# Delta rule: decay differences of four items by one bf16 product of three-part splits

## The reference, cut to what matters

```python
g = -jnp.exp(A_log) * jax.nn.softplus(a + dt_bias)
gc = jnp.cumsum(gT.reshape(Bs, NV, N, CHUNK), axis=-1)
diff = gc[..., :, None] - gc[..., None, :]
decay = jnp.exp(jnp.where(tril, diff, 0.0)) * tril
A = -(jnp.einsum('bhnid,bhnjd->bhnij', k_beta, kc) * decay) * strict
attn = jnp.einsum('bhid,bhjd->bhij', q_i, k_i) * dec_i
```

## Time and profile before

| | |
|---|---|
| median of three executions | 2367.83 us (2364.08 to 2368.61) |
| the profiled execution, its own time | 2367.39 us |
| its span | 2365.6 us |
| phase c in it | about 717 to 1967 us |
| DMA, mean over the span | 30 GB/s |

### The profile page before, as it was taken

How to read it: one execution, slowest core, us unless ns; L and a number is a source line. 1 busy time by engine, 2 the same in 40 slices (tenths; PEclk the granted TensorE clock), 3 DMA queues, 4 the chain that set the end, 5 groups by cost and what they waited for, 6 DMA issues and landing times. The chain is left out here.

```text
span 2365.6 us, 27433 instructions
## 1 busy us (share of the span) xinstructions
PE 2013.7 (85%) x10306; PEld 1495.7 (63%) x10306; DVE 1455.8 (62%) x3243; ACT 879.5 (37%) x1540; POOL 154.4 (7%) x143
## 2 busy tenths in 40 slices
PE   6988987998994978899988999889998893787786
PEld 5867866554553667576675766757667582465464
DVE  3667665323222566867668666786666854767666
ACT  2433433111113444353544535535354431333242
POOL 2011011000001000000000000000000002011110
PEclk8989898999996889999999999999999996787787
DMA  3000000400001110201102011020110202000000
GB/s 131 6 14 10 6 5 30 163 1 9 0 1 67 36 36 14 61 16 36 37 14 57 20 37 36 15 60 17 36 36 14 49 1 72 7 12 15 7 5 5
DMA packets 129108, 70.62 MB, mean 30 GB/s; under 512 B 107152, under 2 KB 119504, under 8 KB 127984
## 3 DMA queue, kind: packets, MB, share of 16 engines
q1 hardware_dynamic: 128976, 68.86, 10.2%
HBM read 55.95 MB, written 12.71 MB: 29 GB/s over the span
## 5 line engine op out<-in xcount | busy, mean ns | idle before, releaser
L1249 PE MATMUL c_bank<-c_Y,c_NP 128*128 128x128 f32 x1536 | 179.5, 276 | 20.9 <-ACT c_Y L1404 20.9
L1249 PEld LDWEIGHTS c_bank<-c_Y,c_NP 128*128 128x128 f32 x1536 | 174.9, 192 | 26.5 <-issue 26.5
L1566 DVE TENSOR_TENSOR c_Y<-c_V,c_bank 128x512 f32<-128x512 f32 x192 | 131.7, 686 | 86.0 <-PE c_bank L1249 86.0
L1541 DVE SCALAR_TENSOR_TENSOR c_NP<-c_NP,c_cj,c_bank 128x256 f32<-128x256 f32 x256 | 104.8, 474 | 69.9 <-ACT c_NP L1411 69.9
L1172 PE MATMUL c_bank<-c_xT,c_wqk 128*128 128x512 f32 x256 | 127.3, 644 | 4.1 <-ACT c_pad L1367 3.1
L1502 DVE SCALAR_TENSOR_TENSOR c_cv<-c_pad,c_wcqk,c_cv 128x1024 f32<-128x1024 f32 x96 | 122.2, 1279 | 11.7 <-ACT c_cv L1381 10.9
L1502 DVE SCALAR_TENSOR_TENSOR c_cv<-c_pad,c_wcv,c_cv 128x1024 f32<-128x1024 f32 x96 | 122.5, 1283 | 2.6
L1327 PE MATMUL c_bank<-c_wout,c_yT 128*128 128x256 f32 x512 | 120.6, 381 | 0.0
L1241 PE MATMUL c_bank<-c_NP,c_Tb 128*128 128x256 f32 x512 | 116.3, 383 | 0.0
L1131 POOL TENSOR_TENSOR c_V<-c_Y 128x512 f32<-128x512 f32 x32 | 40.0, 1249 | 1162.4 <-ACT c_Y L1404 1162.4
L1172 PE MATMUL c_bank<-c_xT,c_wv 128*128 128x512 f32 x256 | 112.0, 595 | 4.1 <-DVE c_acc L1594 3.6
(11 more groups left out here) (401 smaller groups left out, 4147.3 us busy)
## 6 DMA issues: line engine op xcount, KB each, us to landing
b_wup<-b_in_wup SPq DMA_DIRECT2D x4, 1280.0 KB, 14.3
c_wqk<-c_in_wqk SPq DMA_DIRECT2D x9, 512.0 KB, 3.3
c_wv<-c_in_wv SPq DMA_DIRECT2D x8, 512.0 KB, 3.3
c_wz<-c_in_wz SPq DMA_DIRECT2D x8, 512.0 KB, 4.6
c_wout<-c_in_wout SPq DMA_DIRECT2D x8, 512.0 KB, 3.5
diagonal_blocks<-c_NP SPq DMA_DIRECT2D x64, 64.0 KB, 1.9
c_A<-diagonal_blocks SPq DMA_DIRECT2D x8, 512.0 KB, 3.4
c_NP<-no_blocks SPq DMA_DIRECT2D x32, 128.0 KB, 3.8
```

The source lines that it names most:

```text
L1249: last = pe.matmul(banks[n % 4][:, b * P:(b + 1) * P], lhsT(h, 4 * q + b), rhs(h, 4 * q + b), start=True, stop=True)
L1541: dve.scalar_tensor_tensor(NP[:, h, bb, :, :], spread(NP[:, h, bb, 1, :], 2), cj[:, h, bb:bb + 1], gp, ALU.mult, ALU.mult).then_inc(s["NP_ ...
L1566: dve.tensor_tensor(rr(Y, h, q), rr(V, h, q), four(banks[n % 4][:, :]), ALU.subtract).then_inc(s["y_ready"], 1)
```

## The change

The difference of two running sums is now made by one bf16 product. At the start, two f32 products give all running sums (one row for each of the 256 items, in two halves of 128). VectorE splits each f32 sum into three bf16 parts whose sum is the f32 value, and makes the negated parts. They go to DRAM (8 stores). For each round, 16 small loads put them into two SBUF tiles, 16 partitions for each of the 8 units: `row_side` (the moving side, 512 columns: 3 rows of parts of the four items, 12 rows of ones, each over one item's columns) and `col_side` (the weights, one 128x128 for each unit: 3 rows of ones and 12 rows of negated parts of the four items, zero in the other units' rows). One product of the two adds the row sums and subtracts the column sums, in f32, on the mask. So no bias is left in the exponential, and one instruction of 128x512 takes the place of four.

The loads are double buffered by the round's parity. Those of rounds 0 and 1 are issued at the start, that of round i+1 after the scatter of round i.

```diff
-        gcn = sb("gcn", [P, B, VAL_HEADS])
-        gR, gcnR, betaR = (sb(n, [P, HB, B]) for n in ("gR", "gcnR", "betaR"))
+        betaR = sb("betaR", [P, HB, B])
+        gparts = sb("gparts", [P, 2, 2, 3, S], BF16)
+        row_side = sb("row_side", [P, 2, 4 * S], BF16)
+        col_side = sb("col_side", [P, 2, 8, S], BF16)
+        row_base = Y[:, 0].rearrange("p b n -> p (b n)")[:, 0:4 * S]
+        col_base = Y[:, 1]
+        parts = nc.dram_tensor("decay_parts", (2, 2, VAL_HEADS, 4, 3, S), BF16, kind="Internal").ap()
+        SIDE = 16
+        rows_loaded = s["even_rows_loaded"], s["odd_rows_loaded"]
...
+            def load_rows(r):
+                if r >= 2:
+                    sp.wait_ge(s["gcrow_ps"], at(r - 2, 8, 8))
+                for n, (h, q) in enumerate(order):
+                    at0, head = SIDE * n, r * HB + h
+                    sp.dma_start(row_side[at0:at0 + 3, r % 2, :].rearrange("p (b t) -> p b t", b=4),
+                                 parts[0, q, head].rearrange("b p t -> p b t")).then_inc(rows_loaded[r % 2], 16)
+                    sp.dma_start(col_side[at0 + 3:at0 + 15, r % 2, n, :], parts[1, q, head].rearrange("b p t -> (b p) t"))\
+                        .then_inc(rows_loaded[r % 2], 16)
...
+            sp.dma_start(row_base, d["row_side"]).then_inc(s["bases_loaded"], 16)
+            sp.dma_start(col_base, d["col_side"]).then_inc(s["bases_loaded"], 16)
             load_qk(0)
...
             sp.dma_start(no_blocks, Tb[0:BL, :, 0:BL]).then_inc(s["none_stored"], 16)
+            for k in range(2):
+                sp.wait_ge(s["gate_step"], 12 + k)
+                for b in range(4):
+                    sp.dma_start(parts[k, :, :, b].rearrange("q h p t -> h q p t"), gparts[VAL_HEADS * b:VAL_HEADS * b + VAL_HEADS, k])\
+                        .then_inc(s["parts_stored"], 16)
+            sp.wait_ge(s["bases_ready"], 4)
+            sp.wait_ge(s["parts_stored"], 128)
+            load_rows(0)
+            load_rows(1)
             sp.wait_ge(s["none_stored"], 16)
...
                 scatter(i)
+                if 2 <= i + 1 < ROUNDS:
+                    load_rows(i + 1)
...
             pool.memset(ones[:, :], 1.0).then_inc(s["consts"], 1)
+            pool.wait_ge(s["bases_loaded"], 32)
+            for k in range(2):
+                pool.tensor_copy(row_side[:, k, :], row_base).then_inc(s["bases_ready"], 1)
+                pool.tensor_copy(col_side[:, k, :, :], col_base).then_inc(s["bases_ready"], 1)
...
             pe.wait_ge(s["gate_step"], 6)
-            pe.matmul(banks[5][:, 0:B * VAL_HEADS], tri[:, :], flat(g[:, :, :]), start=True, stop=True).then_inc(s["gc_ps"], 1)
+            for q in range(2):
+                last = pe.matmul(banks[3][:, q * S:(q + 1) * S], flat(g[:, 4 * q:4 * q + 4, :]), tri[:, :], start=True, stop=True)
+            last.then_inc(s["gc_ps"], 1)
...
                 if n == 0:
                     pe.wait_ge(s["pad_ready"], at(i, 2 * CHUNKS, 2 * QK))
+                    pe.wait_ge(rows_loaded[i % 2], at(i // 2, 256, 256))
...
                 pe.matmul(four(bank[:, :]), identb[:, :], spread(hiddenb[:, :], 4), start=True, stop=False)
-                for b in range(4):
-                    last = pe.matmul(bank[:, b * P:(b + 1) * P], gR[:, h, 4 * q + b:4 * q + b + 1].broadcast_to([P, P]), tri[:, :],
-                                     start=False, stop=b == 3)
+                last = pe.matmul(bank[:, :], col_side[:, i % 2, n, :], row_side[:, i % 2, :], start=False, stop=True)
                 last.then_inc(s["gcrow_ps"], 1)
...
             def decays_and_grams(r, n):
-                if n == 0:
-                    pe.wait_ge(s["gates_used"], at(r, 3, 3))
...
-            pe.wait_ge(s["gate_step"], 8)
+            pe.wait_ge(s["gate_step"], 7)
...
                 act.wait_ge(s["gcrow_ps"], at(r, 8, n + 1))
-                for b in range(4):
-                    act.activation(NP[:, h, 4 * q + b, 1, :], banks[4 + n % 2][:, b * P:(b + 1) * P], ACT.Exp,
-                                   bias=gcnR[:, h, 4 * q + b:4 * q + b + 1]).then_inc(s["E_ready"], 1)
+                act.activation(NP[:, h, 4 * q:4 * q + 4, 1, :], four(banks[4 + n % 2][:, :]), ACT.Exp).then_inc(s["E_ready"], 4)
...
-            link(dve.tensor_scalar(flat(gcn[:, :, :]), banks[5][:, 0:B * VAL_HEADS], -1.0, None, ALU.mult))
+            gc = banks[3][:, 0:2 * S].rearrange("p (q t) -> p q t", q=2)
+            rest = tmp[:, 0:2 * S].rearrange("p (q t) -> p q t", q=2)
+            link(dve.tensor_copy(gparts[:, 0, :, 0, :], gc))
+            link(dve.tensor_tensor(rest, gc, gparts[:, 0, :, 0, :], ALU.subtract))
+            link(dve.tensor_copy(gparts[:, 0, :, 1, :], rest))
+            link(dve.tensor_tensor(rest, rest, gparts[:, 0, :, 1, :], ALU.subtract))
+            link(dve.tensor_copy(gparts[:, 0, :, 2, :], rest))
+            link(dve.tensor_scalar(gparts[:, 1], gparts[:, 0], -1.0, None, ALU.mult))
...
             def gates(r):
-                for dst, src in ((gR, g), (gcnR, gcn), (betaR, beta)):
-                    dve.tensor_copy(dst[:, :, :], src[:, :, bass.ds(r * HB, HB)].rearrange("p b h -> p h b"))\
-                        .then_inc(s["gates_used"], 1)
+                dve.tensor_copy(betaR[:, :, :], beta[:, :, bass.ds(r * HB, HB)].rearrange("p b h -> p h b")).then_inc(s["gates_used"], 1)
```

More of the change, by code:

```diff
@@ L987, in layer1_delta_rule @@
         g = sb("g", [P, B, VAL_HEADS])
-        gcn = sb("gcn", [P, B, VAL_HEADS])
-        gR, gcnR, betaR = (sb(n, [P, HB, B]) for n in ("gR", "gcnR", "betaR"))
+        betaR = sb("betaR", [P, HB, B])
+        pair = sb("pair", [P, 2])
+        gparts = sb("gparts", [P, 2, 2, 3, S], BF16)
+        row_side = sb("row_side", [P, 2, 4 * S], BF16)
+        col_side = sb("col_side", [P, 2, 8, S], BF16)
         pad = sb("pad", [P, 2, B, TAPS - 1 + S])
@@ L1013, in layer1_delta_rule @@
         blocks = nc.dram_tensor("diagonal_blocks", (2, NBL, ITEMS, BL, BL), F32, kind="Internal").ap()
+        parts = nc.dram_tensor("decay_parts", (2, 2, VAL_HEADS, 4, 3, S), BF16, kind="Internal").ap()
         no_blocks = nc.dram_tensor("no_blocks", (BL, ITEMS, BL), F32, kind="Internal").ap()
-        names = """none_stored blocks_out T_out weights consts pool_step x_loaded xT_ps xT_copied ba_ps gate_step gate_act gc_ps gates_ready
+        names = """none_stored bases_loaded bases_ready parts_stored even_rows_loaded odd_rows_loaded blocks_out T_out weights consts pool_step x_loaded xT_ps xT_copied ba_ps gate_step gate_act gc_ps gates_ready
             qk_loaded v_loaded z_loaded out_loaded gates_used proj_ready pad_ready tap0_ready conv_step cv_ready silu_ready sq_ready norms_ps
@@ L1526, in factors @@
                 link(dve.tensor_tensor(nrm[:, 2], nrm[:, 1], nrm[:, 1], ALU.mult))
-                dve.wait_ge(s["gates_used"], at(r, 3, 3))
+                dve.wait_ge(s["gates_used"], r + 1)
                 for k in range(KB):
@@ L1623, in _ @@
                 dve.wait_ge(s["ln_step"], 3 * b + 1)
-                dve.bn_aggr(gR[:, 0, 0:2], cj[:, 0, 0:6]).then_inc(s["ln_step"], 1)
+                dve.bn_aggr(pair[:, :], cj[:, 0, 0:6]).then_inc(s["ln_step"], 1)
                 dve.wait_ge(s["ln_step"], 3 * b + 2)
-                dve.tensor_copy(f[:, 2, 0:2, b], gR[:, 0, 0:2]).then_inc(s["ln_step"], 1)
+                dve.tensor_copy(f[:, 2, 0:2, b], pair[:, :]).then_inc(s["ln_step"], 1)
                 dve.wait_ge(s["ln_step"], 3 * b + 3)
@@ L1652, in layout_layer1_delta_rule @@
     wqk, wcqk = (np.concatenate([a, a[:1]]) for a in (wqkv.reshape(ROUNDS, P, CHUNKS, DC * P)[:, :, :QK], wconv[:, :, :QK]))
-    return dict(wqk=wqk, wcqk=wcqk, wv=wqkv.reshape(ROUNDS, P, CHUNKS, DC * P)[:, :, QK:], wcv=wconv[:, :, QK:], wz=wz, wout=wout, wba=wba, bias=bias, normw=inp["L1_attn_norm_w"].reshape(P, 1))
+    row_side, col_side = np.zeros((8, 16, 4, S), np.float32), np.zeros((8, 16, 8, S), np.float32)
+    for n in range(8):
+        col_side[n, 0:3, n] = 1.0
+        for b in range(4):
+            row_side[n, 3 + 3 * b:6 + 3 * b, b] = 1.0
+    return dict(row_side=row_side.reshape(P, 4 * S), col_side=col_side.reshape(P, 8, S), wqk=wqk, wcqk=wcqk, wv=wqkv.reshape(ROUNDS, P, CHUNKS, DC * P)[:, :, QK:], wcv=wconv[:, :, QK:], wz=wz, wout=wout, wba=wba, bias=bias, normw=inp["L1_attn_norm_w"].reshape(P, 1))
 LEVELS, QUANT_EPS = 127.0, 1e-8
```

## The result

The changed kernel takes 2323.76 us (median of four runs, 2320.99 to 2325.44) where the kernel before takes 2367.94 beside it: 0.9832 of it, 95% interval 0.9816 to 0.9847. That is 44.2 us less; the forecast was 43.9 less. The profiled execution took 2323.68 us around a span of 2321.7.

What follows compares the result with a forecast made beforehand. The prediction took the latency of a TensorE, ScalarE and VectorE ring in the delta-rule stage as the bound. Seven rounds 37.8, round 0 5.6 and set-up 0.5 sum to 43.9 us less: 2324 us, range 2312 to 2345.

Steps and rivals of the forecast that it cites:

- What bounds the kernel: Delta-rule stage, run eight times: the latency of a ring of TensorE, ScalarE and VectorE bounds it, no engine being full.
- The differences: TensorE, per unit: mask product plus one bf16 product, 1.11 to 0.43 us, 0.68 less, 64 times.
- The exponential: ScalarE, per unit: one of 128x512 without per-partition operand takes 0.60 us where four took 1.14.
- The rival's price for an exponential that stays at 1.14: Decay stage: if exponentials still cost 1.14 us, about 34 us gained in all, 2334; no chance of its own.
- Pace: VectorE's products in the ring: first to third 5.16 to 3.95 us, first to seventh 19.38 to 16.2, 3.2 less.
- The head: Stage start up to VectorE's first product: 1.8 us earlier in round 1, 2.2 in the mean of seven rounds.
- rival 1: Stage: clock rises later, head gives 1.1; output products take back 1.4 of 3.2; 25.4 us gained, 2342; chance 0.21.
- Rival 2: Ring: clock stays at 1.2 GHz from head to first output product, so slower, 2383 us; chance 0.05.
- Round 0: Stage without output products: 2.0 us in the head and three pairs at 1.2, together 5.6 us.
- The set-up: First projection no longer waits for negated sums, starts about 0.5 us earlier; VectorE's split lies in a wait.
- SP's queue: Sixteen small loads a round at 0.57 to 0.90 us each, 9 to 14.4 in all; nothing on the path.
- The sum: Whole kernel: 37.8 + 5.6 + 0.5 = 43.9 us gained; 34 to 54 us had chance 0.66.

Runs made afterwards that it cites:

- both_back: Changed kernel with three idle repeats of the mask product per unit and four exponentials with a zero per-partition bias: 2363.88 us, 1.0002 of the kernel before.
- zero_bias: Changed kernel with four 128x128 exponentials a unit and a per-partition bias of zeros: 2330.99 us, 0.9860 of the kernel before.
- changed_again: The changed kernel unaltered, measured on another occasion beside the kernels compared with it: 2322.65 us, 0.9818 of the kernel before.
- four_exps: Changed kernel with four 128x128 exponentials a unit in place of one, still without bias: 2321.38 us, 0.9826 of the kernel before.
- fill_before_norms: Changed kernel with six mask products whose result nobody reads put before the one-column norm products: 2317.91 us, 0.9799 of the kernel before.
- early_pairs: pair_order with the differences of units 0 and 1 also issued ahead of TensorE's wait for the norms: 2304.16 us, 0.9740 of the kernel before.
- pair_order: Changed kernel with two units' differences issued before their two grams (units 0 to 3, 6 and 7; all in round 0): 2306.62 us, 0.9754 of the kernel before.

## Why the prediction was right, step by step

**What bounds the kernel** held: both_back puts only two durations back and brings back the time of before. **The differences** (1.11 to 0.43 us) are as forecast: 1063.56 to 1063.78, 0.22, and the second product 0.38 with its tail.

**The exponential** was forecast at 0.60 and measured 0.596, but the reason was half told. The prediction saw that the new one has no per-partition operand and took the row without one for it; what it did not see is that this, and not the width, is most of the gain: 8.9 of 11.6 us in the stretch. The rival's price for an exponential that stays at 1.14, 34 us gained in all, is zero_bias: 35 by the times.

**Pace.** Third product after the first: forecast 3.95, measured 4.00 (and 0.78 us idle before it, where 0.6 to 0.7 was said: a little above). Seventh after the first: forecast 16.2, measured 16.38, so 3.0 a round and not 3.2. The 0.2 is the first error of size: seven rounds, 1.4 us.

**The head.** Forecast 1.8 us in round 1 and 2.2 in the mean of seven, from the first mask product to VectorE's first product. Read so, round 1 went from 5.99 us to 4.37, 1.6 less, and the mean from 6.57 to 4.34, 2.2 less. What the layout for round 1 had wrong is the clock, which it took to rise as long after the first mask product as before; it did not:

```profile
1054.00:1057.00 3.00, 3.00 (x15) 2.68 (x16) 0.21 (x2) 0.30 (x2) 0.00 (x0) 0.50 0.00 0
1057.00:1060.00 3.00, 3.00 (x9) 2.00 (x8) 1.61 (x8) 1.89 (x3) 0.00 (x0) 0.50 0.00 0
1060.00:1061.00 1.00, 1.00 (x5) 0.80 (x4) 0.11 (x1) 0.60 (x1) 0.00 (x0) 0.63 0.00 0
1061.00:1066.00 5.00, 3.90 (x16) 1.91 (x14) 4.22 (x11) 1.37 (x3) 0.00 (x0) 1.00 0.00 0
```

In these windows of the changed kernel (columns as in the earlier trace rows) 1054 to 1060 is at 0.50, 1.2 GHz, and the rise to 2.4 comes in 1060 to 1061, some 4.2 us after the first mask product where it was 3.1. That cost the missing 0.2. The clock also fell earlier, 2.6 us ahead of the first mask product where it was 0.3, and so the one-column products, which the forecast left alone, took 4.80 us up to it (1051.72 to 1056.52) where they took 3.73. Counted from the last group of one-column products, the head of round 1 gained only about 0.5 us (9.7 to 9.2), and the mean of seven 2.1 (10.90 to 8.79 in changed_again). In the other six rounds the time at 1.2 GHz lasts as long after the change as before it, the shorter products are worth twice as much in it, and all six gained 1.8 to 3.0. In the mean of seven that time is 5.9 us before and 6.3 after: the premise of rival 1, that the clock rises later with less work, came true in one round of seven, and its size did not. Its other half fell too. TensorE's output products took nothing back: the 3.0 us of the pace are all there from VectorE's first product to the next projection (34.11 to 31.11).

**Rival 2**, the clock down in the ring, fell: 1061 to 1066 is at 1.00 with TensorE busy for 3.90 of 5 us, so the ring's gaps of 0.8 us in each pair left the clock at its upper level. The sentence of the Trainium skill, "TensorE: Matmul & The Clock Gate", Part 1: The HAM clock gate, that activity releases the throttle, read as the prediction read it, would have gone with 2383 us; this trace does not bear that reading out. The prediction also misread one row for this rival: the one-column products fill the window 768 to 774 from 768.12 on, not from its middle; its 0.69 means that the clock was down for its last 3.7 us.

**Round 0.** Products every 4.00 us (784.63, 788.63, 792.63, 796.63) in place of 5.16: 3 times 1.16 as forecast, and 2.0 in the head (9.76 to 7.79). With the way to the projection that is 5.3 us measured, 5.6 forecast. **The set-up.** The first projection now waits for the reciprocal of beta, 0.56 us idle before it where 1.02 was: 0.46 of the 0.5 forecast. Not all of it arrives. Counted from the phase's first product, the projection starts 0.45 us earlier (20.26 to 19.81), but its first sixteen products take 9.90 us where they took 9.67, and the one-column products start 0.22 earlier (40.26 to 40.04). VectorE's split runs beside the projection, and nothing waits for it:

```profile
746.14 1.75 DVE L1523 RECIPROCAL c_beta<-c_A 128x256 f32<-128x256 f32 x1
...
747.95 9.90 PE L1210 MATMUL c_bank<-c_xT,c_wqk 128*128 128x512 f32 x16 [0.56 <-DVE c_beta L1523]
...
749.96 0.36 DVE L1532 TENSOR_SCALAR c_gparts<-c_gparts 128x768 bf16<-128x768 bf16 x1
```

**SP's queue.** Right in the sum, wrong in the price: the 0.57 to 0.90 us per issue came from large scattered transfers, the small row loads take 0.34 each, sixteen 5.4 us. The wv load has 7.5 us left after them, so the "1.5 us later" end of the forecast was too dark. The rows of rounds 0 and 1 are issued by 765.4, and TensorE's first mask product (780.27) waits for none. In the changed kernel's queue:

```profile
978.30 0.45 SPq L1085 DMA_DIRECT2D c_row_side<-decay_parts  x1
978.78 0.30 SPq L1087 DMA_DIRECT2D c_col_side<-decay_parts  x1
...
983.40 0.30 SPq L1087 DMA_DIRECT2D c_col_side<-decay_parts  x1
991.18 0.36 SPq L1055 DMA_DIRECT2D c_wv<-c_in_wv  x1
```

**One wait not foreseen:** the table load ahead of the first exponential now begins after the first difference product, 0.61 us idle (1057.62), 5.0 us in eight rounds. In the kernels with four exponentials per unit (before, four_exps, zero_bias, both_back) it is 0.1 in all, so the wait came with the single instruction; its reason is open. It is off the path, because VectorE's first product needs exponential 1, which waits 0.69 us for its own product (1060.19).

**The sum** was 37.8 for seven rounds, 5.6 and 0.5. In changed_again the stretch is 42.7 us shorter: 5.3 in round 0 and 37.4 in the seven others, 5.3 each. The pace's 3.0 and the head's 2.1 make 5.1 of it; the 0.2 left lies, by subtraction, ahead of the point from which the head is read. With the 0.2 of the set-up that arrives that is 42.9 us, and the medians of three comparisons give 44.2, 43.4 and 42.0. That the first of them agrees with 43.9 to a third of a microsecond is luck within the scatter; the terms agree to about a microsecond.

What stays open is the low clock around the head, some 6 us a round at half speed: neither fill_before_norms nor the products that early_pairs puts ahead of the one-column ones took it away, and why it was shorter in pair_order was not tested.

## What to carry to other kernels

In a ring of engines in which none is full, price each link by its latency and not by its engine's busy time: 42 us of TensorE work put back cost 30, because only some of the differences lie on the path, and 8.9 of the time saved on ScalarE came from an operand, not from fewer instructions. Before merging small activations, see whether their per-partition bias can be folded into a product that runs anyway: here that was most of ScalarE's gain, and the merging little. And once a ring is bound by latency, look at the order of issue first, since two units' differences ahead of their grams gave another 14 to 20 us with no work taken out. When a kernel's scatter is 5 us, time the stretch that the change touches from the trace, between two events that all versions have, and confirm the cause by putting the durations back.

## What the runs showed that was not expected

A per-partition bias operand costs 85 ns on each activation (368 against 283 ns for 128x128 out of PSUM), whether it holds values or zeros. Issues of 3 KB loads on SP take 0.34 us each, not the 0.57 to 0.90 of the large scattered ones. One 512-wide exponential in place of four moves the wait for its data ahead of the table load. And six full-width products ahead of the one-column norm products left the head as it was (8.84 against 8.79 us), at 1.2 GHz.
